# Split value products, transfers to head strips, and a new engine order in six local-attention layers

## The chip, the cores and the metric

The kernel runs on one core of a Trainium2 chip. The core has TensorE (PE in the profile; its weight loads are PEld), VectorE (DVE), ScalarE (ACT), GpSimd (POOL) and SyncE (SP), which here only issues transfers. Each has its own instruction stream, and they meet at semaphores. The metric is device time in microseconds of one launch.

## The reference

A layer norm of x (2 sequences of 1024 rows, 128 wide) feeds two branches, whose results are added to x. One is a causal attention with 8 heads over 2 latent key/value groups (the global attention). The other is six local layers, one after the other. Cut to what matters, a local layer is:

```
qkv = shift_tokens(x) @ Wqkv                      # 128 -> 3 * 1024, 16 heads of 64
q, k = l2norm(q) * qs, l2norm(k) * ks             # then rotary, with a scale that grows with the row
sim = 8 * q . k                                   # a block of 32 rows sees its own block and the one before
attn = softmax(where(mask, -max, sim))
x = (attn @ v).reshape(b, n, 1024) @ Wo + x
xn = layernorm(shift_tokens(x)) * g + b
a, gate = split(xn @ W1 + b1)                     # 128 -> 2 * 341
x = (a * gelu(gate)) @ W2 + b2 + x
```

## The kernel before

All data of a sequence lies in SBUF. The global attention comes first (some 270 us); then a loop over steps G runs the six local layers, 16 tiles of 128 rows each, as a pipeline: each engine has its own list of functions that it calls in step G, each for a tile G - 1, G - 2 and so on, and every wait is a semaphore written by hand. The order inside each list is the order of calls in the last loop of each engine's block. A few functions work on chunks of four tiles: `chunk_at(G, 10)` names the chunk whose turn it is in step G, so the feed-forward's work falls in steps 10 to 13 after the chunk began, and recurs every four steps.

A tile passes these stations. TensorE projects queries and keys (`projected`: each 512 columns are three matmuls, upper x upper, upper x lower, lower x upper, of fp32r parts). ScalarE squares them (`square_keys`, `square_queries`), VectorE multiplies by the rotary tables `tabs` (`cosine`, `sine`) and sums the squares; POOL adds the two rotary parts, makes the seeds of the inverse roots (`seeds`, `refine`), and scales (`scale_keys`, `scale_queries`). TensorE transposes keys, queries and later the probabilities through banks 2 and 3 (`transposes`), ScalarE copies them out. `scores` adds the products onto a mask in banks 4 and 5, VectorE takes maxima and subtracts them, ScalarE exponentiates, VectorE sums, POOL scales.

Values. The weights of values and output are folded for each layer into M (`products`, `folded_upper`), so that the values of a head are already 128 wide. `values(k, g)` makes 64 of a tile's 128 rows in each of two calls: 32 rows at a time, the four heads' groups q land on the four partition strips of 32 in banks 4 and 5, in plain fp32. So ScalarE's `copy_values` puts them in `vw` where `weigh` needs them: strip q holds heads of group q, a block of 32 rows in the free dimension. `vw` is a ring of six half tiles.

Keys. `kT` holds 32 columns of look-back ahead of the tile's 128; POOL's `lookback` copies the last 32 to the front for the next tile.

Rows of the feed-forward. VectorE's `attended` adds the attention to the residual `Xt`; SyncE's `rows_in_place` moves these rows, one half shifted down by one row, to `lns` in three transfers; VectorE's `moments` takes their statistics and `normalise_rows` writes `lnx`; TensorE transposes it (`ln_columns`), ScalarE copies it twice (`xnf`, and `xnH` rounded), POOL subtracts (`lower_columns`). `up_gate`, `up_value`, `gelu`, `gated` and `down` are the feed-forward. The gelu needs another activation table than Ln and Exp, so that ScalarE loads tables before and after.

SyncE's list is one queue. In the local layers it holds, for each tile, the three transfers of rows, and for each layer the weights.

## Time and profile before

| | us |
|---|---|
| median of 3 runs | 1753.11 |
| lowest, highest | 1746.89, 1754.92 |
| the profiled execution | 1745.55 |
| its span, first to last instruction | 1743.9 |
| busy in it: TensorE, VectorE | 1619.5, 1495.5 |
| busy in it: POOL, ScalarE | 1340.6, 1318.4 |
| mean granted TensorE clock | 0.984 |

Busy is the time in which an engine had at least one instruction in work; a matmul's end is modelled. The rows further down are from the profiled execution. A step of the pipeline is one tile on each engine.

### The profile page before, as it was taken

To read this page: it belongs to the slowest core of one execution; us is meant where nothing else is said; L and a number is where in the kernel's file an instruction comes from. 1 tells how busy PE (TensorE), PEld (TensorE's weight loads), DVE (VectorE), ACT (ScalarE), POOL (GpSimd) and SP (SyncE) were. 2 spreads that over 40 slices of the span, in tenths; PEclk is the share of its full clock that TensorE was granted. 3 is DMA by queue.
4 is the path that set the end of the run, shared out by engine and by line. 5 is a ranking of instruction groups with operands and counts; after the bars stand their busy time and mean duration, and the time that the engine had idled before them with its cause. 6 is when DMAs were issued, how large, how long until landed. Compare 5 with 4: busy or idle time off the path is not lost.

```text
span 1743.9 us, 72603 instructions
## 1 busy us (share of the span) xinstructions
PE 1619.5 (93%) x31192; PEld 1098.7 (63%) x31192; DVE 1495.5 (86%) x1863; ACT 1318.4 (76%) x1934; POOL 1340.6 (77%) x1311
## 2 busy tenths in 40 slices
PE   6999978889999999999998999999999999999995
PEld 4777855556566666665665666666666666666654
DVE  5677857999889998898998888999999988999982
ACT  3788846687787788778777877877887887788773
POOL 2312159888988899988888888899888998888871
PEclk8999989999999999999999999999999999999997
DMA  5221100100001000011000010000010000000001
GB/s 158 67 50 39 38 1 30 35 7 8 15 7 59 6 8 12 16 31 34 8 12 14 8 57 7 7 12 15 7 59 7 12 6 15 8 7 7 8 7 28
DMA packets 47997, 40.61 MB, mean 23 GB/s; under 512 B 33216, under 2 KB 41152, under 8 KB 46016
## 3 DMA queue, kind: packets, MB, share of 16 engines
q1 hardware_dynamic: 47680, 35.98, 7.4%
q8 instruction: 249, 4.08, 0.9%
q14 instruction: 68, 0.56, 0.1%
HBM read 20.22 MB, written 1.05 MB: 12 GB/s over the span
## 4 chain that ended last, share of the span: by engine, by line
PE 51%; DVE 22%; issue 13%; ACT 8%; POOL 6%; DMA 0%; SPq 0%; DVEq 0%; POOLq 0%; ACTq 0%
PE banks L1205 23%; PE banks L1494 9%; PE banks L1443 5%; PE banks L1518 4%; DVE arena L1066 4%; PE banks L1479 4%; PE banks L1335 4%; DVE lnx L1128 3%; DVE small L1095 3%; DVE small L1101 2%; DVE small L1089 2%; DVE small L1113 2%; DVE arena L1061 2%; ACT arena L807 1%; ACT L873 1%
## 5 line engine op out<-in xcount | busy, mean ns | idle before, releaser
L1494 PE MATMUL banks<-M,xs 128*32 128x512 f32 x3072 | 368.0, 596 | 0.6 <-ACT arena L807 0.3
L1061 DVE TENSOR_TENSOR arena<-banks,tabs 128x1024 f32<-128x1024 f32 x192 | 233.8, 1218 | 35.5 <-ACT arena L767 22.4
L548 POOL TENSOR_TENSOR arena<-arena 128x1024 f32<-128x1024 f32 x96 | 229.8, 2393 | 43.7 <-DVE arena L1066 43.3
L807 ACT ACTIVATE arena<-banks 128x1024 f32<-128x1024 f32 x192 | 197.0, 1026 | 68.3 <-PE banks L1494 67.6
L1066 DVE TENSOR_TENSOR arena<-banks,tabs 128x1024 f32<-128x1024 f32 x192 | 233.2, 1215 | 0.0
L553 POOL TENSOR_TENSOR arena<-arena 128x1024 f32<-128x1024 f32 x96 | 228.3, 2378 | 0.0
L543 POOL TENSOR_TENSOR prob<-prob,small 128x1024 f32<-128x1024 f32 x96 | 184.0, 1916 | 30.0 <-DVE small L1103 30.0
L1128 DVE SCALAR_TENSOR_TENSOR lnx<-lns,small 128x128 f32<-128x128 f32 x96 | 175.3, 1826 | 34.2 <-POOL small L596 32.8
L1205 PE MATMUL banks<-qkH,xsH 128*128 128x512 f32 x384 | 173.1, 451 | 32.1 <-DVE arena L1066 29.2
L1518 PE MATMUL banks<-arena 128*32 128x128 f32 x6144 | 190.9, 277 | 5.6 <-ACT arena L873 4.2
L608 POOL TENSOR_TENSOR arena<-arena,small 128x1024 f32<-128x1024 f32 x96 | 182.9, 1906 | 9.8 <-POOL arena L553 0.4
L602 POOL TENSOR_TENSOR arena<-arena,small 128x1024 f32<-128x1024 f32 x96 | 182.9, 1905 | 7.5
L767 ACT ACTIVATE arena<-banks 128x1024 f32<-128x1024 f32 x96 | 98.3, 1024 | 113.6 <-PE banks L1205 113.4
L1479 PE MATMUL banks<-arena 64*32 64x64 f32 x12288 | 147.2, 226 | 32.0 <-issue 17.0
L1518 PEld LDWEIGHTS banks<-arena 128*32 128x32 f32 x6144 | 164.5, 111 | 12.4 <-issue 6.0
L1479 PEld LDWEIGHTS banks<-arena 64*32 64x32 f32 x12288 | 130.1, 105 | 58.4 <-issue 56.8
L1494 PEld LDWEIGHTS banks<-M,xs 128*32 128x32 f32 x3072 | 88.4, 110 | 123.2 <-issue 116.2
L1205 PEld LDWEIGHTS banks<-qkH,xsH 128*128 128x128 f32 x384 | 73.2, 191 | 132.8 <-issue 110.0
L1205 PE MATMUL banks<-qkL,xsH 128*128 128x512 f32 x384 | 153.6, 400 | 2.4 <-issue 2.4
L1205 PE MATMUL banks<-qkH,xsL 128*128 128x512 f32 x384 | 153.7, 400 | 0.0
L778 ACT ACTIVATE arena<-banks 128x1024 f32<-128x1024 f32 x96 | 98.4, 1025 | 72.0 <-PE banks L1205 71.8
L1443 PEld LDWEIGHTS banks<-cst,arena 64*128 64x128 f32 x3072 | 111.5, 139 | 61.8 <-issue 41.9
(134 smaller groups left out, 3645.4 us busy)
## 6 DMA issues: line engine op xcount, KB each, us to landing
qkraw<-in_wqk_dram SPq DMA_DIRECT2D x6, 1024.0 KB, 5.2
arena<-in_wvo_dram SPq DMA_DIRECT2D x5, 1024.0 KB, 5.4
gq<-w1w SPq DMA_DIRECT2D x64, 64.0 KB, 2.0
lns<-Xt SPq DMA_DIRECT2D x96, 32.0 KB
lns<-Xt SPq DMA_DIRECT2D x96, 31.8 KB
xsH<-w1w SPq DMA_DIRECT2D x32, 64.0 KB, 2.0
xsL<-w1w SPq DMA_DIRECT2D x32, 64.0 KB, 2.0
W<-in_w_dram SPq DMA_DIRECT2D x6, 341.0 KB, 3.2
```

Of the source, the lines that this page charges most:

```text
L543: pool.tensor_tensor(p, p, d, ALU.mult).then_inc(s["p_nrm"], 1)
L548: pool.tensor_tensor(kc, kc, ks, ALU.add).then_inc(s["k_add"], 1)
L553: pool.tensor_tensor(qc, qc, qs, ALU.add).then_inc(s["q_add"], 1)
L807: act.activation(vw[:, (2 * k + g) % RV, :], two(V_BANK), ACT.Copy).then_inc(s[f"v_cp{g}"], 1)
L1061: dve.tensor_tensor(heads(c), heads(two(0)), table(k % NT, kind), ALU.mult).then_inc(s[done], 1)
L1066: dve.tensor_tensor(w.rearrange("p (h z k) -> p h z k", h=LH, z=2), swapped(two(0)), table2(k % NT, kind + 1), ALU.mult).then_inc(s[done], 1)
L1128: dve.scalar_tensor_tensor(lnx[:, :], lns[:, k % 2, :], ag[:, k % 2, 0:1], rs[:, 4, 32:33].to_broadcast([P, D]), ALU.subtract, ALU.mult).t ...
L1205: return pe.matmul(o, l, r, start=start, stop=stop)
L1443: ins = pe.transpose(bk(2 + o)[:, 64 * k:64 * (k + 1)], src[r, P * k:P * (k + 1)], ident[r, r])
L1479: ins = pe.matmul(bk(4 + o)[WIN * w:WIN * (w + 1), 64 * j:64 * (j + 1)], qT[r, j, WIN * w:WIN * (w + 1)], kT[r, j, WIN * w:WIN * w + 64], ...
L1494: ins = pe.matmul(bk(V_BANK + z)[WIN * q:WIN * (q + 1), :], xs[:, b, t0:t0 + WIN], M[:, q, :, :].rearrange("p m n -> p (m n)"), start=True ...
L1518: ins = pe.matmul(bk(PV_BANK)[WIN * w:WIN * (w + 1), 0:D], ptile[:, NQ * z + m, WIN * w:WIN * (w + 1)], block_of(k, w - 1 + z)[:, D * m:D ...
```

## The change

It moves several things at once, all in the local layers.

Values: the folded weights are kept as an upper and a lower fp32r part (MH, and ML in the place of a buffer of the global attention); VectorE's `folded_lower` makes the lower part. `values(k, g)` now makes all 128 rows of half of the head groups, in six matmuls of 128x512. Its result has rows on partitions, so ScalarE copies it to `vst`, and SyncE moves it to the strips of `vw` by 16 transfers a tile, each of 32 partitions and 2 KB a partition (`place_values`). `weigh` waits for these.

```diff
             def values(k, g):
...
+                pe.wait_ge(s["xs_L"], k // 4 + 1)
+                pe.wait_ge(s["M_L"], 2 * (k // TILES) + 2)
                 claim(V_BANK, V_BANK + 1)
+                xH, xL = xsH[:, b, P * i:P * (i + 1)], xsL[:, b, P * i:P * (i + 1)]
                 for z in range(2):
-                    t0 = P * i + 64 * g + WIN * z
-                    for q in range(NQ):
-                        ins = pe.matmul(bk(V_BANK + z)[WIN * q:WIN * (q + 1), :], xs[:, b, t0:t0 + WIN],
-                                        M[:, q, :, :].rearrange("p m n -> p (m n)"), start=True, stop=True, skip_group_check=True)
+                    mH, mL = (a[:, 2 * g + z, :, :].rearrange("p m n -> p (m n)") for a in (MH, ML))
+                    mm(bk(V_BANK + z), xH, mH, True, False)
+                    mm(bk(V_BANK + z), xH, mL, False, False)
+                    ins = mm(bk(V_BANK + z), xL, mH, False, True)
...
             def copy_values(k, g):
                 act.wait_ge(s[f"v_mm{g}"], k + 1)
-                after(act, "o_mm", k - 2 + g)
-                act.activation(vw[:, (2 * k + g) % RV, :], two(V_BANK), ACT.Copy).then_inc(s[f"v_cp{g}"], 1)
+                if k:
+                    act.wait_ge(v_in[g], P * k)
+                act.activation(vst[:, g, :], two(V_BANK), ACT.Copy).then_inc(s[f"v_cp{g}"], 1)
...
+            def place_values(k, g):
+                if k <= LAST_TILE:
+                    sp.wait_ge(s[f"v_cp{g}"], k + 1)
+                    after(sp, "o_mm", k - 1)
+                    for q in range(2 * g, 2 * g + 2):
+                        for w in range(NW):
+                            sp.dma_start(block_of(k, w)[WIN * q:WIN * (q + 1), :], vst[WIN * w:WIN * (w + 1), g, CH * (q % 2):CH * (q % 2 + 1)])\
+                              .then_inc(v_in[g], 16)
...
+            def folded_lower(l, r):
+                dve.wait_ge(s["M_H"], 2 * l + r + 1)
+                m = [a.rearrange("p q (o r) n -> p o q r n", r=2)[:, :, :, r, :] for a in (MH, ML)]
+                dve.tensor_tensor(m[1], two(2).rearrange("p (o q n) -> p o q n", o=2, q=NQ), m[0], ALU.subtract).then_inc(s["M_L"], 1)
```

The transposes that share banks 2 and 3 with the folded weights now wait for M_L in the place of M_H. SyncE's order in a tile becomes:

```diff
+                place_values(k + 2, 0)
                 rows_in_place(k)
+                place_values(k + 2, 1)
+                load_table(k + 3)
```

`load_table` fetches one piece of the rotary table anew in the second half of each layer, since the table is now scaled in place and has no copy (this makes room for `vst`).

Rows and columns of the feed-forward: the normalisation goes from VectorE to ScalarE, with a small product (`row_shifts`) on POOL ahead of it; the lower part of the columns goes from POOL to VectorE, which reads the bank, so that the copy `xnf` is gone.

```diff
+            def normalise_rows(k):
+                if is_tile(k):
+                    act.wait_ge(s["row_mr"], k + 1)
+                    after(act, "lnB_mm", k)
+                    act.activation(lnx[:, :], lns[:, k % 2, :], ACT.Identity, bias=nmr[:, k % 2:k % 2 + 1], scale=rs[:, 4, 32:33])\
+                       .then_inc(s["ln_x"], 1)
...
-                    dve.scalar_tensor_tensor(lnx[:, :], lns[:, k % 2, :], ag[:, k % 2, 0:1],
-                                             rs[:, 4, 32:33].to_broadcast([P, D]), ALU.subtract, ALU.mult).then_inc(s["ln_x"], 1)
+            def lower_columns(k):
+                if is_tile(k):
+                    at, f = k % 4 * P, k // 4 % 2
+                    dve.wait_ge(s["xn_H"], k + 1)
+                    dve.tensor_tensor(xnL[f][:, at:at + P], bk(6)[:, 0:P], xnH[f][:, at:at + P], ALU.subtract).then_inc(s["xn_L"], 1)
```

Keys: `kT` becomes a ring of six blocks of 32; `scores` reads pairs of neighbouring blocks from it (`key_pair`), and POOL's copy is gone, but for clearing one block at the start of a sequence.

The orders of the lists: the three gate projections of a chunk come in the same step and use banks 6, 7, 7, the three gelus follow each other on ScalarE between one pair of table loads, `moments` goes from the head of VectorE's step to its end, and `weigh` and `values_lower` go from the head of TensorE's step to the end of the one before, which changes nothing in the row of instructions.

```diff
-LAST_GELUS = (1, 2,)
+GATE_BANK, VALUE_BANK = (6, 7, 7), (6, 7, 6)
+LAST_GELU = 2
```

TensorE, from the transpose of the normalised rows to the scores of a tile, in a step with projections up. `cst,lnx` is that transpose, `cst,arena` that of the queries, `cst,prob` that of the probabilities. Before:

```order
L1536 MATMUL banks<-cst,lnx 128x128
L1443 MATMUL banks<-cst,arena 128x64 x16
L1494 MATMUL banks<-M,xs 32x512 x8
L1205 MATMUL banks<-xnw,w1w 128x512 x3
L1443 MATMUL banks<-cst,prob 128x64 x16
```

Now (`gq` is ML, and `w1w` here is the fourth quarter of the columns):

```order
L1600 MATMUL banks<-cst,lnx 128x128
L1498 MATMUL banks<-cst,arena 128x64 x16
L1260 MATMUL banks<-MH,xsH 128x512
L1260 MATMUL banks<-gq,xsH 128x512
L1260 MATMUL banks<-MH,xsL 128x512
L1260 MATMUL banks<-MH,xsH 128x512
L1260 MATMUL banks<-gq,xsH 128x512
L1260 MATMUL banks<-MH,xsL 128x512
L1260 MATMUL banks<-xnw,w1w 128x512 x2
L1260 MATMUL banks<-w1w 128x512
L1498 MATMUL banks<-cst,prob 128x64 x16
```

The values' half went from eight matmuls of 32 rows to six of 128, and both kinds are followed by the feed-forward's products as before.

SyncE, in the middle of a layer, where a new sequence begins (`zrow` is its empty row). Before, two tiles:

```order
L354 DMA lns<-Xt 127x64 [waits ln_x,x1]
L358 DMA lns<-zrow 1x16x4 [waits zeroed]
L359 DMA lns<-Xt 128x64
L354 DMA lns<-Xt 127x64 [waits ln_x,x1]
L358 DMA lns<-Xt 1x16x4
```

Now, one tile with a table piece behind it:

```order
L414 DMA arena<-vst 32x512 [waits o_mm,v_cp0]
L414 DMA arena<-vst 32x512 x7
L359 DMA lns<-Xt 127x64 [waits ln_x,x1]
L363 DMA lns<-Xt 1x16x4
L364 DMA lns<-Xt 128x64
L414 DMA arena<-vst 32x512 [waits o_mm,v_cp1]
L414 DMA arena<-vst 32x512 x7
L405 DMA tabs<-in_tab_dram 128x256 [waits tab,q_s]
```

The three transfers of rows stand between two groups of eight, and a piece of the table behind them.

ScalarE, around the gelus. L873 and L910 are `gelu`, L767 and L796 `square_keys`, L802 and L833 `copy_probs`. Before (the third gelu has a pair of loads of its own, at the end of the step):

```order
L802 ACTIVATE arena<-banks 128x1024
L873 ACT_TABLE_LOAD
L873 ACTIVATE arena<-banks,b1p 128x512
L767 ACTIVATE arena<-banks 128x1024
L873 ACTIVATE arena<-banks,b1p 128x512
L876 ACT_TABLE_LOAD
L840 ACTIVATE prob<-prob 128x1024
```

Now:

```order
L910 ACT_TABLE_LOAD
L910 ACTIVATE arena<-banks,b1p 128x512
L833 ACTIVATE arena<-banks 128x1024
L910 ACTIVATE arena<-banks,b1p 128x512
L796 ACTIVATE arena<-banks 128x1024
L910 ACTIVATE arena<-banks,b1p 85x512
L913 ACT_TABLE_LOAD
```

All three gelus stand between two loads, from the end of one step to the head of the next.

## Rows read from the trace of the kernel before

**Rows 1.** The page: busy us of each engine, and the chain that ended last.

```profile
PE 1619.5 (93%) x31192; PEld 1098.7 (63%) x31192; DVE 1495.5 (86%) x1863; ACT 1318.4 (76%) x1934; POOL 1340.6 (77%) x1311
...
PE 51%; DVE 22%; issue 13%; ACT 8%; POOL 6%; DMA 0%; SPq 0%; DVEq 0%; POOLq 0%; ACTq 0%
```

**Rows 2.** Busy us by window: PE, PEld, DVE, ACT, POOL, then clock, DMA, GB/s.

```profile
500.00:750.00 250.00, 241.02 (x4899) 158.23 (x4892) 231.67 (x272) 202.35 (x264) 223.64 (x215) 1.00 0.07 18
```

**Rows 3.** Timeline (start, duration, instruction), VectorE: first tile, and 80 tiles later.

```profile
276.60 0.28 DVE L1108 TENSOR_TENSOR Xt<-banks,Xt 128x128 f32<-128x128 f32 x1
...
1499.44 0.28 DVE L1108 TENSOR_TENSOR Xt<-banks,Xt 128x128 f32<-128x128 f32 x1
```

**Rows 4.** Timeline of TensorE through one step of the local layers.

```profile
589.81 1.90 PE L1494 MATMUL banks<-M,xs 128*32 128x512 f32 x16
591.64 0.50 PE L1205 MATMUL banks<-qkH,xsH 128*128 128x512 f32 x1
...
593.14 0.27 PE L1536 MATMUL banks<-cst,lnx 128*128 128x128 f32 x1
...
593.98 1.92 PE L1494 MATMUL banks<-M,xs 128*32 128x512 f32 x16
595.83 2.94 PE L1205 MATMUL banks<-W,arena 128*128 128x128 f32 x24
...
602.27 0.60 PE L1582 MATMUL banks<-cst,Xt 128*128 128x128 f32 x4
...
605.22 0.61 PE L1494 MATMUL banks<-M,xs 128*32 128x512 f32 x4
```

**Rows 5.** Timeline of TensorE, one up projection.

```profile
580.87 0.96 PE L1205 MATMUL banks<-xnw,w1w 128*128 128x512 f32 x3
```

**Rows 6.** Groups: count, busy us, mean ns, then idle before and its releaser.

```profile
L548 POOL TENSOR_TENSOR arena<-arena 128x1024 f32<-128x1024 f32 x96 | 229.8, 2393 | 43.7 <-DVE arena L1066 43.3
...
L1128 DVE SCALAR_TENSOR_TENSOR lnx<-lns,small 128x128 f32<-128x128 f32 x96 | 175.3, 1826 | 34.2 <-POOL small L596 32.8
...
L1119 DVE TENSOR_TENSOR prob<-banks,small 128x1024 f32<-128x1024 f32 x96 | 117.6, 1225 | 10.3 <-DVE small L1113 0.5
...
L873 ACT ACT_TABLE_LOAD x46 | 59.0, 1283 | 2.3 <-PE banks L1205 1.5
...
L559 POOL TENSOR_TENSOR xnw<-xnf,xnw 128x128 fp32r<-128x128 f32 x96 | 44.1, 459 | 5.0 <-ACT xnw L854 5.0
...
L570 POOL COPY arena<-arena 128x256 f32<-128x256 f32 x84 | 38.0, 452 | 9.2 <-PE banks L1479 8.9
...
L1108 DVE TENSOR_TENSOR Xt<-banks,Xt 128x128 f32<-128x128 f32 x96 | 26.9, 281 | 7.3 <-PE banks L1518 7.2
...
L853 ACT ACTIVATE xnf<-banks 128x128 f32<-128x128 f32 x96 | 26.1, 271 | 5.2 <-PE banks L1536 5.2
```

**Rows 7.** Timeline of VectorE at the end of the kernel.

```profile
1724.05 0.34 DVE L1128 SCALAR_TENSOR_TENSOR lnx<-lns,small 128x128 f32<-128x128 f32 x1
```

**Rows 8.** Timeline of SyncE's queue in the global attention: 16 transfers, and 16 more.

```profile
167.44 2.41 SPq L371 DMA_DIRECT2D xsH<-w1w  x4
169.90 3.23 SPq L371 DMA_DIRECT2D xsL<-w1w  x4
173.17 5.02 SPq L371 DMA_DIRECT2D gq<-w1w  x8
182.21 2.41 SPq L371 DMA_DIRECT2D xsH<-w1w  x4
...
187.19 6.12 SPq L371 DMA_DIRECT2D gq<-w1w  x8
```

**Rows 9.** Timeline of SyncE's queue in a local layer: the rows of one tile.

```profile
608.89 0.63 SPq L354 DMA_DIRECT2D lns<-Xt  x1
...
610.46 0.59 SPq L359 DMA_DIRECT2D lns<-Xt  x1
```

**Rows 10.** The page, DMA issues: count, KB each, us from issue to landing.

```profile
gq<-w1w SPq DMA_DIRECT2D x64, 64.0 KB, 2.0
```

More of the change, by code:

```diff
@@ L125, in build @@
         xs = sb("xs", [P, B, T + 1])
-        xnw = sb("xnw", [P, 4 * CH], F32R)
-        xnH, xnL = (xnw[:, 2 * CH * i:2 * CH * (i + 1)].rearrange("p (f n) -> p f n", f=2) for i in range(2))
-        M = sb("M", [P, NQ, NQ, D])
+        xnw = sb("xnw", [P, 3 * CH], F32R)
+        quarters = [xnw[:, CH * i:CH * (i + 1)] for i in range(3)] + [w1w[:, 4 * FF:4 * FF + CH]]
+        xnH, xnL = quarters[0:2], quarters[2:4]
+        MH = sb("MH", [P, NQ, NQ, D], F32R)
         gq2 = sb("gq2", [P, 2, T], F32R)
-        gK = [xnw[:, T * z:T * (z + 1)] for z in range(2)]
+        ML = gq2.rearrange("p z t -> p (z t)").rearrange("p (q m n) -> p q m n", q=NQ, m=NQ)
+        vst = sb("vst", [P, 2, 2 * CH])
+        gK = [quarters[0:2], quarters[2:4]]
         gQ = [xsH[:, 1, 0:T], xsL[:, 1, 0:T], gq2[:, 0, :], gq2[:, 1, :]]
@@ L153, in build @@
         gag = small[:, 466:498].rearrange("p (t k) -> p t k", k=2)
+        nmr = small[:, 498:500]
         lns = sb("lns", [P, 2, D])
@@ L223, in build @@
         rows_in = [sem("rows_in0"), sem("rows_in1")]
+        v_in = [sem("v_in0"), sem("v_in1")]
         lat_w, lat_wq, lat_k, out_in = (sem(n) for n in ("lat_w", "lat_wq", "lat_k", "out_in"))
@@ L389, in _, with load_table @@
                     place_queries(it, z)
+            sp.wait_ge(s["gK_lo"], 2 * B * KV)
+            sp.wait_ge(s["gQ_lo"], 2 * B * KV)
+            sp.dma_start(tabs[:, NT // 2:NT, :], tab_d[:, NT // 2:NT, :]).then_inc(tab_in, 16)
+            def load_table(k):
+                l, n = divmod(k, TILES)
+                if 0 <= k <= LAST_TILE and n >= NT and l + 1 < DEPTH:
+                    sp.wait_ge(s["q_s"], k + 1)
+                    sp.wait_ge(s["tab"], NT * (l + 1) + n - NT)
+                    sp.dma_start(tabs[:, n - NT, :], tab_d[:, n - NT, :]).then_inc(tab_in, 16)
+            def place_values(k, g):
[6 more added lines that the diff above has]
+                              .then_inc(v_in[g], 16)
             out_t = out.rearrange("b (t p) d -> p (b t) d", p=P)
+            for k in range(2):
+                for g in range(2):
+                    place_values(k, g)
             for k in range(LAST_TILE + 1):
@@ L787, in copy_keys @@
                     act.wait_ge(s["kT_mm"], k + 1)
-                    act.wait_ge(s["look"], k + 1)
-                    act.activation(kT[:, :, WIN:WIN + P].rearrange("p k (o t) -> p k o t", o=2), halves(2), ACT.Copy)\
-                       .then_inc(s["kT_cp"], 1)
+                    after(act, "s_mm", k)
+                    first = NW * k % KB // 2
+                    at = kT.rearrange("p k (o t) -> p k o t", t=2 * WIN)
+                    at = at[:, :, 2::-2, :] if first == 2 else at[:, :, first:first + 2, :]
+                    act.activation(at, halves(2), ACT.Copy).then_inc(s["kT_cp"], 1)
             def copy_queries_T(k):
@@ L1033, in _ @@
             add_outputs(PAIRS - 2)
-            dve.memset(gl[2][64:128, :], 1.0).then_inc(s["ones"], 1)
             dve.memset(rin[:, :, :], 1.0).then_inc(s["ones"], 1)
-            dve.wait_ge(s["ones"], 2)
             def heads(a):
@@ L1133, in moments @@
                     dve.wait_ge(rows_in[k % 2], 48 * (k // 2) + 48)
+                    after(dve, "row_mr", k - 1)
+                    after(dve, "ln_x", k - 1)
                     dve.bn_stats(st6[:, :], lns[:, k % 2, :]).then_inc(s["ln_bn"], 1)
@@ L1510, in weigh @@
                     pe.wait_ge(s["pt_cp"], k + 1)
-                    pe.wait_ge(s["v_cp0"], k + 1)
-                    pe.wait_ge(s["v_cp1"], k + 1)
+                    for g in range(2):
+                        pe.wait_ge(v_in[g], P * (k + 1))
                     pe.wait_ge(s["vw_0"], 1)
@@ L1556, in up_value, with down, down_first @@
                     up(c, j, FJ[j][0], f"a_mm{j}")
-                    freed[6 + j % 2] = (f"h{j}", c + 1)
-            def down(c):
+                    freed[VALUE_BANK[j]] = (f"h{j}", c + 1)
+            def down(c, tiles):
+                for t in tiles:
+                    for j in range(3):
+                        m = FJ[j][1] + (j == 2)
+                        ins = mm(bk(DN_BANK)[:, P * t:P * (t + 1)], gl[j][0:m, P * t:P * (t + 1)], W2[0:m, c // NC % 2, j, :], j == 0, j == 2)
+                return ins
+            def down_first(c):
                 if c is not None:
@@ L1564, in down, with down_last @@
                     claim(DN_BANK)
-                    for t in range(4):
-                        for j in range(3):
-                            m = FJ[j][1] + (j == 2)
-                            ins = mm(bk(DN_BANK)[:, P * t:P * (t + 1)], gl[j][0:m, P * t:P * (t + 1)], W2[0:m, c // NC % 2, j, :], j == 0, j == 2)
-                    ins.then_inc(s["f_mm"], 1)
+                    down(c, (0, 1))
                     freed[DN_BANK] = ("x_new", c + 1)
+            def down_last(c):
+                if c is not None:
+                    down(c, (2, 3)).then_inc(s["f_mm"], 1)
             def next_shifts(c):
```

177 lines of the change are left out of this document (92 added, 85 removed).

## The prediction

> **What bounds the kernel now.** I read the page's busy shares and its chain first [rows 1]. TensorE is busy 93% of the span, VectorE 86%, POOL 77%, ScalarE 76%; the chain that ended last runs through TensorE for 51% of the span, through VectorE for 22%, and another 13% is "issue". So no engine alone sets the pace. TensorE does it for most of the time and VectorE where TensorE has to wait for it.
>
> Then the stages. In 250 us from the middle of the local layers [rows 2] TensorE works 241.0, VectorE 231.7, POOL 223.6, ScalarE 202.4. Three engines are within 7% of the stretch. The pace itself is read from the addition that ends the attention of a tile (VectorE L1108, once a tile): it starts at 276.60 for the first tile and at 1499.44 five layers of 16 tiles later [rows 3]. That is 1222.84 / 80 = 15.3 us a tile, on average. The local layers fill some 1460 of the 1744 us; what lies ahead (the global attention) is hardly touched by the change.
>
> What TensorE must do in a tile is read off one full step of its program, from the lower values at 589.81 to the next ones at 605.22 [rows 4]: 15.41 us without a hole. In it lie the down projection (2.94 us) and the layer transposes (0.60 us), which come once in four tiles; since the end of a group runs 0.07 us into the next one (591.64 against 589.81 + 1.90), they occupy 2.87 and 0.53 us; without them a step holds 12.0 us. One up projection is 0.96 - 0.07 = 0.89 us [rows 5], and six come in four tiles. So a tile costs 12.0 + (2.87 + 0.53 + 6 x 0.89) / 4 = 14.2 us on average, and the weight products and bias columns at a layer's edge (about 3.5 us in 16 tiles, an estimate from the 24 small products of the down projection in 2.87 us) make it 14.4. Against 15.3 that leaves **0.9 us a tile in which TensorE waits**.
>
> **The change part by part.**
>
> Values. The two halves of a tile's values take 591.64 - 589.81 = 1.83 and 595.83 - 593.98 = 1.85 us now [rows 4]. The new code makes each half of six 128x512 products on the same operands' shapes and types as a projection, and a projection of six takes 593.14 - 591.64 = 1.50 us. So TensorE gains 0.33 + 0.35 = 0.68 us a tile: 96 x 0.68 = **65 us**, all of it on the engine that sets the pace. New TensorE content: 14.4 - 0.7 = 13.7 us a tile.
>
> VectorE. L1128 leaves it: 1826 ns on average, 175 us in all [rows 6]. Its size (128x128) is that of L1108 at 281 ns [rows 6], so most of it is standing still. At the very end of the kernel, where POOL has nothing left, it takes 0.34 us [rows 7]; I read the rest as a wait for POOL. The new L1164 (lower part of the normalised columns) has one operand in PSUM and is of the form of L1108: 0.28 us. The lower parts of the folded weights add 12 instructions of the size of L1119, 1.2 us each, 0.15 us a tile. VectorE goes from 231.7 / 250 x 15.3 = 14.2 us a tile to 14.2 - 1.83 + 0.28 + 0.15 = **12.8**.
>
> POOL loses L559 (459 ns) and 84 copies of L570 (452 ns, 0.40 us a tile) and gets a one-column instruction that no row shows; it lies between 0 and the 0.46 of L559, and I take 0.25: 223.6 / 250 x 15.3 = 13.7 goes to **13.1**. ScalarE loses the second copy of the columns (L853, 271 ns) and gets the normalisation of a 128x128 tile: the same size, so nothing. The table loads fall from 92 around the gelus to 46: 46 x 1.283 = 59 us [rows 6], 0.6 us a tile, so ScalarE goes from 12.4 to **11.8**. That counts above all in the step that held all three gelus and four loads.
>
> The Trainium skill, ScalarE: Activation LUTs, section "What ACT_TABLE_LOAD costs", puts a switch to another set at 2.66 us, the load of 1283 ns with a drain of 1380 ns. The load agrees with this trace (1283 ns); for the drain the trace has no row. By the page 46 switches would be 122 us of ScalarE, by the rows 59.
>
> SyncE gets the real bill: 16 transfers of 64 KB a tile, where it had three small ones. The global attention issues exactly that pattern (16 transfers, 32 partitions by 2 KB): 167.44 to 178.19 and 182.21 to 193.31 [rows 8], so 10.75 and 11.1 us, **0.68 us each** with the long one among them. The three row transfers last from 608.89 to 611.05, 2.2 us [rows 9]. A table piece in every second tile and the weight loads add 0.3 + 0.25 us. Together 10.9 + 2.2 + 0.55 = 13.7 us a tile. It fits below 14.3, with little to spare, and it does not run ahead: the first eight wait for the ScalarE copy of the lower half, the second eight stand behind the rows, which wait for the residual addition. Laid out by hand from the order of the program and the durations above, with the end of the query projection as 0: lower half copied at about -0.3, its eight issued by 5.3, rows by 7.5, upper eight by 13.0, table piece by 13.6. The statistics of those rows now stand at the end of VectorE's step, at about 13, and the rows have landed by 10 (a 64 KB transfer lands in 2.0 us [rows 10]); the weighing that needs the values comes some 8 us after they landed. So SyncE's own work is hidden as long as one issue stays at 0.68. The transfers themselves move 1 MB in 14 us; in the global attention the same 1 MB went in 11 [rows 8], so bandwidth is not the matter.
>
> What is late next. With VectorE and ScalarE relieved, TensorE waits for POOL's chain (rotate, scale, seeds), which is 13.1 of 14.3 us. Three gate projections now lie in one step and one in the next (TensorE's four steps become 11.3 + 2.7 = 14.0, 11.3 + 0.9 = 12.2, 11.3 + 1.8 = 13.1 and 11.3 + 3.4 = 14.7 us), so in the light step POOL or SyncE paces and in the heavy ones they catch up. I take a third of the 0.9 us of waiting as gone: 0.3 us in 80 tiles, **24 us**. The bounds are nothing (0) and nearly all of it (0.75 x 80 = 60).
>
> Costs of the edges. Before the transposes at a layer's edge TensorE used to wait for ScalarE's copy of the folded weights; now VectorE's lower part comes behind it, 1.2 us, and about 1 us of it shows: 5 us. At the entry two such instructions and the first transfers: 3 to 5 us, taken as 4. The ring of key blocks takes the place of POOL's copy with no instruction of its own; the key copy keeps its size. Bounds of these small things: -2 to +15 us.
>
> Sum: 65 + 24 - 5 - 4 = 80. The profiled execution took 1745.55 us (span 1743.9), so 1745.6 - 80 = **1666 us**. That execution is 0.4% below the median 1753.11; the shown runs reach from 1746.9 to 1754.9, and I keep to the profiled one.
>
> **The rivals.**
>
> All waiting goes. If the 0.9 us were nearly all VectorE's doing (the chain gives it 22%), TensorE runs through: 1745.6 - 65 - 60 + 5 = 1626 us. Against it: POOL at 13.1 and SyncE at 13.7 do not let 13.7 through evenly.
>
> SyncE paces, mildly. If an issue costs 0.72 to 0.77 us in this traffic, SyncE needs 11.5 to 12.3 + 2.75 = 14.3 to 15.1 us and the tile follows it: 1680 to 1740 us. For it: the rows put it at 13.7 already, and each handshake (copy done, residual done) adds some tenths that the global attention didn't have.
>
> SyncE paces, and the kernel gets slower. One group of four in the trace took 3.23 us (0.81 each) [rows 8]. If that were the usual price, 16 x 0.81 + 2.75 = 15.7 us, and with some 0.4 us of handshakes 16.1: 0.8 us a tile over now, 77 us, **about 1820 us**. It decides from 15.3 us a tile, that is from about 0.76 us an issue with the handshakes. Place: the second eight stand behind the rows on SyncE, then ScalarE's upper copy waits for their landing and TensorE for that copy. Against it: only one in eight to sixteen issues was long in the global attention.
>
> The change does nothing. POOL's chain of 13.1 us plus its waits for k_s and the denominators would hold 15.2 us; then 1740 to 1750. Little speaks for it, since POOL's largest idle, 43.7 us before L548, ends with VectorE's L1066 [rows 6], and VectorE comes earlier now.
>
> **How the numbers follow.** Forecast as summed, 1640 to 1695 us: 0.50. All waiting gone, 1610 to 1640: 0.12. SyncE mildly, 1695 to 1740: 0.20. Same: 0.05. Slower: 0.13. What a measurement of this kernel can tell from no change is about 0.5%. So faster 0.82, same 0.05, slower 0.13. The range 1622 to 1740 leaves out the slower case, the same and the end of the best one.
>
> **What would show it.** In the profile after: six value products in 1.5 us between starts; L1128's 175 us gone from VectorE and the new lower columns at about 0.28 us; 46 table loads fewer; 16 transfers issued in about 11 us a tile on SyncE, with a short idle behind them; the addition after attention every 14.3 us. The forecast is wrong if TensorE or ScalarE waits for the landing of values (v_in), if VectorE's statistics wait for rows, or if the light step (one gate product, the third in four) is as long as the others.

## The result, and the profile after

The changed kernel takes 1766.07 us (median of 5 runs, 1763.87 to 1768.14) against 1753.11 before. The ratio of runs made side by side is 1.008, with a 95% interval of 1.0061 to 1.010: slower by 0.8%, where 1666 us was forecast with a range of 1622 to 1740. The profiled execution took 1768.14 us, its span is 1766.4, and the mean granted TensorE clock is 0.964 (0.984 before).

The page of the changed kernel, to be held against [rows 1]: busy us of each engine, the chain that ended last, and the granted clock in 40 slices.

```profile
PE 1592.2 (90%) x29272; PEld 1260.5 (71%) x29272; DVE 1363.8 (77%) x1875; ACT 1274.8 (72%) x1888; POOL 1294.2 (73%) x1227
...
PEclk8999998999999999999999999999999999999997
...
PE 70%; ACT 10%; issue 9%; DVE 4%; POOL 3%; SPq 3%; DMA 1%; ACTq 0%; POOLq 0%; DVEq 0%
```

Every engine has less to do: TensorE 27 us less, VectorE 132, POOL 46, ScalarE 44. TensorE's share of the chain rose from 51 to 70% and VectorE's fell from 22 to 4%. So the relief is there, and the profiled span is still 22.5 us longer. The same stretch as [rows 2] (PE, PEld, DVE, ACT, POOL busy, clock, DMA share, GB/s):

```profile
500.00:750.00 250.00, 233.10 (x4622) 185.30 (x4607) 205.97 (x265) 192.21 (x255) 214.02 (x197) 0.99 0.37 91
```

TensorE works 233 of 250 us where it had worked 241. Where it stands, the groups say (count, busy us, mean ns, then the idle time ahead and what ended it). First the scores in the kernel before:

```profile
L1479 PE MATMUL banks<-arena 64*32 64x64 f32 x12288 | 147.2, 226 | 32.0 <-issue 17.0 <-ACT banks L822 11.9
```

and in the changed one, with the weighing, the normalisation, the lower columns, a table load and the copy of the values:

```profile
L1582 PE MATMUL banks<-arena 128*32 128x128 f32 x6144 | 198.7, 284 | 2.1 <-DVE arena L1202 1.5 <-issue 0.4
...
L839 ACT ACTIVATE vst<-banks 128x1024 f32<-128x1024 f32 x192 | 196.7, 1025 | 75.6 <-PE banks L1260 71.7 <-DMA arena<-vst 3.5
L1542 PE MATMUL banks<-arena 64*32 64x64 f32 x12288 | 162.9, 227 | 90.7 <-issue 48.9 <-ACT banks L854 41.6
...
L890 ACT ACTIVATE lnx<-lns,small 128x128 f32<-128x128 f32 x96 | 46.1, 480 | 0.8 <-POOL small L598 0.7
...
L910 ACT ACT_TABLE_LOAD x23 | 29.5, 1283 | 0.4
...
L1164 DVE TENSOR_TENSOR xnw<-banks,xnw 128x128 fp32r<-128x128 f32 x48 | 13.5, 281 | 2.2 <-ACT xnw L884 2.2
```

Idle ahead of a score product went from 32.0 to 90.7 us. It has two parts. 41.6 us end with L854, ScalarE's copy of the mask into banks 4 and 5: TensorE is at the scores before the mask is. And 48.9 us are "issue": TensorE stands in the middle of the 128 products of a tile and waits for no engine. One such place, in the timeline of the changed kernel's TensorE (start, duration, instruction):

```profile
1284.02 0.39 PE L1260 MATMUL banks<-qkH,xsL 128*128 128x512 f32 x1
1284.25 0.39 PE L1260 MATMUL banks<-qkH,xsH 128*128 128x512 f32 x1
...
1288.79 0.71 PE L1498 MATMUL banks<-cst,prob 64*128 64x64 f32 x16
1289.92 1.42 PE L1542 MATMUL banks<-arena 64*32 64x64 f32 x109 [0.41 <-ACT banks L854]
1293.82 0.60 PE L1542 MATMUL banks<-arena 64*32 64x64 f32 x19 [2.49 <-issue]
1294.35 0.79 PE L1260 MATMUL banks<-qkH,xsH 128*128 128x512 f32 x1
1294.94 0.63 PE L1260 MATMUL banks<-qkL,xsH 128*128 128x512 f32 x1
1295.37 0.63 PE L1260 MATMUL banks<-qkH,xsL 128*128 128x512 f32 x1
```

The probabilities' transposes, then 0.41 us for the mask, 109 score products in 1.42 us, a stop of 2.49 us, the other 19. Behind the stop the same projection product comes every 0.43 us where it came every 0.23 us ahead of it (1284.02, 1284.25). The windows ahead of and behind the stop:

```profile
1281.00:1285.00 4.00, 4.00 (x56) 3.16 (x45) 4.00 (x5) 3.94 (x6) 3.44 (x2) 1.00 0.36 86
...
1293.80:1297.20 3.40, 3.38 (x26) 2.56 (x27) 2.45 (x2) 0.00 (x0) 3.04 (x2) 0.51 0.36 81
```

The granted clock went from 1.00 to 0.51, the upper and the lower of the two levels of 2.4 and 1.2 GHz. I counted both from the records of the local layers. Stops of over 0.3 us within the scores: 14 with 17.0 us before, 25 with 48.9 us after. Stretches at the lower clock: 3 with 10.2 us together before, 19 with 71.7 us after; ahead of 17 of these 19 TensorE had just stood for over 0.9 us. Half of 71.7, some 36 us, is my estimate of the time lost there, against 5 us before.

The last place is SyncE's queue (timeline, changed kernel): eight transfers of values, then the rows of one tile; the next eight transfers stand behind these.

```profile
1303.51 5.91 SPq L414 DMA_DIRECT2D arena<-vst  x8
1309.51 0.66 SPq L359 DMA_DIRECT2D lns<-Xt  x1
1310.22 0.84 SPq L363 DMA_DIRECT2D lns<-Xt  x1
1311.10 1.05 SPq L364 DMA_DIRECT2D lns<-Xt  x1
```

Eight in 5.91 us are 0.74 us each here; over all 1536 the mean is 0.65 (median 0.59, and 124 of them over 0.9 us). In a steady stretch SyncE is occupied about 14.2 of 15.5 us a tile, the short pauses between issues counted in (13.1 us in the issues alone). ScalarE waited 3.5 us in the whole kernel for landed values (L839 above).

### The profile page after: what moved, and what is told of

The parts are those of the page before. It is cut to its first block, busy times and chain, and to the rows that moved or that the text cites. A ratio compares the mean times of both kernels' runs of the same rounds, so it can differ in the third digit from the quotient of the medians.

```text
span 1766.4 us, 70552 instructions
## 1 busy us (share of the span) xinstructions
PE 1592.2 (90%) x29272; PEld 1260.5 (71%) x29272; DVE 1363.8 (77%) x1875; ACT 1274.8 (72%) x1888; POOL 1294.2 (73%) x1227
## 4 chain that ended last, share of the span: by engine, by line
PE 70%; ACT 10%; issue 9%; DVE 4%; POOL 3%; SPq 3%; DMA 1%; ACTq 0%; POOLq 0%; DVEq 0%
PE banks L1260 41%; PE banks L1582 9%; PE banks L1542 8%; PE banks L1498 7%; PE banks L1390 4%; ACT vst L839 4%; ACT banks L854 3%; SPq L414 2%; POOL arena L631 1%; POOL arena L586 1%; POOL arena L637 1%; DMA arena<-vst 1%; DVE gq L1169 0%; DVE small L1131 0%; PE banks L1600 0%
## 5 line engine op out<-in xcount | busy, mean ns | idle before, releaser
L1149 DVE TENSOR_REDUCE small<-banks 128x16 f32<-128x1024 f32 x96 | 117.6, 1225 | 185.1 <-PE banks L1542 185.1
L796 ACT ACTIVATE arena<-banks 128x1024 f32<-128x1024 f32 x96 | 98.5, 1027 | 216.5 <-PE banks L1260 216.4
L839 ACT ACTIVATE vst<-banks 128x1024 f32<-128x1024 f32 x192 | 196.7, 1025 | 75.6 <-PE banks L1260 71.7
L1542 PE MATMUL banks<-arena 64*32 64x64 f32 x12288 | 162.9, 227 | 90.7 <-issue 48.9
L1542 PEld LDWEIGHTS banks<-arena 64*32 64x32 f32 x12288 | 142.6, 106 | 104.8 <-issue 100.8
L576 POOL TENSOR_TENSOR prob<-prob,small 128x1024 f32<-128x1024 f32 x96 | 184.3, 1919 | 31.8 <-DVE small L1139 31.5
L1582 PE MATMUL banks<-arena 128*32 128x128 f32 x6144 | 198.7, 284 | 2.1 <-DVE arena L1202 1.5
L1260 PE MATMUL banks<-MH,xsH 128*128 128x512 f32 x384 | 172.4, 449 | 0.5 <-ACT vst L839 0.5
L1260 PE MATMUL banks<-MH,xsL 128*128 128x512 f32 x384 | 152.0, 396 | 0.0
L1260 PE MATMUL banks<-gq,xsH 128*128 128x512 f32 x384 | 151.5, 395 | 0.0
L1498 PE MATMUL banks<-cst,arena 64*128 64x64 f32 x3072 | 142.8, 235 | 7.3 <-POOL arena L631 3.0
```

The lines of the kernel that those rows point to most:

```text
L576: pool.tensor_tensor(p, p, d, ALU.mult).then_inc(s["p_nrm"], 1)
L839: act.activation(vst[:, g, :], two(V_BANK), ACT.Copy).then_inc(s[f"v_cp{g}"], 1)
L1260: return pe.matmul(o, l, r, start=start, stop=stop)
L1498: ins = pe.transpose(bk(2 + o)[:, 64 * k:64 * (k + 1)], src[r, P * k:P * (k + 1)], ident[r, r])
L1542: ins = pe.matmul(bk(4 + o)[WIN * w:WIN * (w + 1), 64 * j:64 * (j + 1)], qT[r, j, WIN * w:WIN * (w + 1)], key_pair(r, j, NW * k + w - 1), ...
L1582: ins = pe.matmul(bk(PV_BANK)[WIN * w:WIN * (w + 1), 0:D], ptile[:, NQ * z + m, WIN * w:WIN * (w + 1)], block_of(k, w - 1 + z)[:, D * m:D ...
```

## The experiments

All were timed beside the kernel before; its medians were 1751.35 us beside e1, e3 and e4, 1749.01 beside e5 to e8 and 1752.15 beside e9 to e12. In the table "stops" and "mask" are the idle us ahead of a score product that end with "issue" and with the mask copy, from the groups of each profile, and "low clock" is the us of local layers at the lower level. The ratios carry the comparisons between rows; e8, e9, e10 and e12 were run four times each, the others nine or ten times. The last three columns are from one execution of each kernel, and some of these lie off the median: e3's took 1773.59 us, e5's 1733.04, e8's 1717.74, e9's 1778.37, e10's 1777.22 and e11's 1745.71.

| | median us | ratio to before [95%] | stops | mask | low clock |
|---|---|---|---|---|---|
| before | | 1 | 17.0 | 11.9 | 10.2 |
| changed | 1766.07 | 1.008 [1.0061, 1.0100] | 48.9 | 41.6 | 71.7 |
| e1 no transfers | 1747.75 | 0.9969 [0.9937, 1.0001] | 45.3 | 37.5 | 68.3 |
| e3 old values | 1760.96 | 1.0039 [1.0012, 1.0067] | 31.2 | 44.8 | 61.4 |
| e4 padding | 1766.18 | 1.0079 [1.0055, 1.0104] | 51.6 | 38.5 | 81.9 |
| e5 tiny transfers | 1748.11 | 0.9987 [0.9956, 1.0019] | 32.7 | 38.9 | 44.4 |
| e6 old gates | 1748.37 | 0.9984 [0.9959, 1.0009] | 39.1 | 23.1 | 51.2 |
| e7 old values, old gates | 1755.74 | 1.0033 [1.0012, 1.0053] | 26.7 | 19.9 | 37.5 |
| e8 transposes first | **1725.54** | **0.987 [0.9815, 0.9926]** | 17.4 | 35.5 | 30.7 |
| e9 before, adjacent | 1771.29 | 1.0102 [1.0052, 1.0153] | 25.9 | 15.5 | 23.9 |
| e10 before, first | 1785.3 | 1.0186 [1.0134, 1.0237] | 21.2 | 11.3 | 27.3 |
| e11 old values, first | 1750.57 | 0.9996 [0.9965, 1.0026] | 19.6 | 35.9 | 34.1 |
| e12 no transfers, first | 1710.22 | 0.9771 [0.9726, 0.9816] | 20.3 | 29.2 | 37.5 |

The first question was whether the 16 transfers, the new values or the rest of the change took the gain.

**e1: the changed kernel without the transfers.** ScalarE copies straight into `vw`. The values then stand in the wrong strips; what each engine computes keeps its size.

```diff
             def copy_values(k, g):
...
-                act.activation(vst[:, g, :], two(V_BANK), ACT.Copy)
+                after(act, "o_mm", k - 2 + g)
+                act.activation(vw[:, (2 * k + g) % RV, :], two(V_BANK), ACT.Copy)
...
-                place_values(k + 2, 0)
                 rows_in_place(k)
-                place_values(k + 2, 1)
```

> The changed kernel without the 16 transfers a tile: ScalarE copies the values straight to the ring, so the rows of the values stand in the wrong strips (the output is not the reference's); TensorE's matmuls are the same in number and size. Two things may have cost the forecast gain. Theory SyncE: issuing and landing of the transfers (TensorE's waits ahead of the scores grew from 5.5 to 33.8 us, and ScalarE's staging copies wait for landings). Theory pauses: TensorE stops in the middle of the score matmuls right behind a 16 KB fetch of its instructions (9 stops, 17 us before; 19 stops, 46 us after) and runs at half clock for 3.4 us after each (3 such stretches before, 19 after). If SyncE alone: the 28 us and what hangs on it go, 1766 to about 1735, and the stops stay at 19. If the stops come from the traffic of the transfers: they fall to 9 or fewer and the time to 1670 to 1685, near the forecast of 1666. If the stops come from where fetches fall in the instruction stream: they stay, whatever the transfers.

1747.75 us, 18 less than the changed kernel. The transfers cost something, but without them 65 us of TensorE's work and the relief of three engines are still worth only 0.3%, with an interval that just reaches nothing. Stops and mask waits are nearly those of the changed kernel, and 21 of the 25 stops come in the same tile at the same product. They belong to the program, not to the transfers.

**e3: the changed kernel with the values of before** (plain fp32, no transfers, no lower parts of the folded weights).

```diff
-                    mm(bk(V_BANK + z), xH, mH, True, False)
-                    mm(bk(V_BANK + z), xH, mL, False, False)
-                    ins = mm(bk(V_BANK + z), xL, mH, False, True)
+                    t0 = P * i + 64 * g + WIN * z
+                    for q in range(NQ):
+                        ins = pe.matmul(bk(V_BANK + z)[WIN * q:WIN * (q + 1), :], xs[:, b, t0:t0 + WIN],
+                                        M[:, q, :, :].rearrange("p m n -> p (m n)"), start=True, stop=True, skip_group_check=True)
```

> The changed kernel with the values of before (plain fp32, 32 rows at a time, straight into the ring; no folded lower parts, no transfers): all the rest of the change alone. By the forecast's terms the rest (rows on ScalarE, key ring, gelus grouped) brings 24 us of TensorE's waiting and costs nothing at the edges: about 1725 to 1730. If the rest of the change is at fault (order of the gates, key ring), it is at 1750 or more. Theory pauses by the place in the stream: the instruction count of a tile is that of before again, so the number of stops returns to about 9.

1760.96 us. The rest of the change alone costs some 7 us by the ratio (10 by the medians), where I had it as a gain of 24. So the new values with all that belongs to them cost 7 us on top (ratios 1.0080 and 1.0039; 5 by the medians), in place of giving 65.

**e4: 128 waits that are already fulfilled, on TensorE ahead of the local loop.** If the stops came from where the program's pieces happen to begin, shifting it would change their number.

```diff
+            for _ in range(128):
+                pe.wait_ge(s["xs_L"], 1)
             for G in range(STEPS):
                 project_queries(G - 1)
```

> The changed kernel with 128 already fulfilled semaphore waits on TensorE ahead of the local loop, at its start: this shifts all later fetches of its instructions against the matmuls, and costs 5 us or less once. If the stops in the scores depend on where a fetch falls in the stream, their number and the time move clearly (by 10 us or more, either way). If they come from the traffic of transfers, both stay: 19 stops, 1766 to 1771 us.

1766.18 us, the time of the changed kernel. The stops moved to other products, mostly of other tiles, and their sum stayed (51.6 against 48.9 us). So the position in the stream decides which product is hit, but an unlucky position isn't what made them many.

**e5: e1 with 16 tiny transfers a tile**, 32 rows of 64 bytes, with the same waits and semaphores.

```diff
+                            sp.dma_start(dm[WIN * q:WIN * (q + 1), 16 * w:16 * (w + 1)], vw[WIN * w:WIN * (w + 1), (2 * k + g) % RV, CH * (q % 2):CH * (q % 2) + 16])\
+                              .then_inc(v_in[g], 16)
```

> The kernel without transfers, to which 16 tiny ones a tile are added again, each 32 partitions by 64 bytes into a tile that nobody reads, with the same waits for them on ScalarE and TensorE (the values stand in the wrong strips, so the output is not the reference's). SyncE then has the changed kernel's queue, but the megabyte is gone. The kernel without transfers ran in 1747.75 us, the changed one in 1766. If issues and their waits make the 18 us, this is at 1760 to 1768; if the bytes make them (the score matmuls take 1.59 us at the median with transfers, 1.41 without), it is at 1745 to 1752 with scores at 1.41.

1748.11 us, the same as e1 (1747.75), each with some 5 us of uncertainty. So SyncE's issues and their handshakes cost nothing that these runs can tell; the 18 us are the price of the bytes. (e2, a first form of this with the real transfers made narrow, gave no time.)

**e6: the changed kernel with the gates' places of before.** The third gate product comes one step later; it and the third value product stand again between the probabilities' transposes and the scores; the third gelu has its own table loads at the end of the step.

```diff
                 up_value(chunk_at(G, 12), 1)
-                up_value(chunk_at(G, 12), 2)
                 up_gate(chunk_at(G, 10), 0)
...
                 transpose_probs(G - 3)
+                up_value(chunk_at(G, 12), 2)
+                up_gate(chunk_at(G, 11), 2)
                 scores(G - 2)
...
-                up_gate(chunk_at(G, 10), 2)
```

> The changed kernel with the feed-forward's products in the places of before: the third gate one step later, and it and the third value product between the transposes of the probabilities and the scores, on ScalarE the third gelu at the end of the step with table loads of its own. Theory place: with a slow run of products ahead of the scores, TensorE neither waits for the mask at their start (63 waits over 0.3 us in the changed kernel, 38.9 us; 11.9 us before) nor stops so long within them (48.9 against 17.0 us), so it falls to 1700 to 1730 us although ScalarE gets 46 table loads more. Rival: the stops come with the new values (fewer, denser instructions); then it stays within 1750 to 1770, and the table loads cost what little the waits gave.

1748.37 us: 18 less, although ScalarE has 59 us of table loads more again. Both kinds of idle time ahead of score products fell. The regrouping that was to help ScalarE is what costs these 18 us.

**e7: e3 and e6 together.** What is left of the change is the normalisation on ScalarE, the lower columns on VectorE, the statistics at the step's end and the ring of key blocks.

> As the last, but with the values of before too (plain fp32, no transfers): what is left of the change is the rows on ScalarE, the lower columns on VectorE, the key ring and the moved statistics. By the forecast they give about 24 us against the kernel before (1751): 1725 to 1730. If place is what costs in the run with old values alone (1761), this is at or below 1735; if the key ring or the moved statistics cost, it stays at 1750 or more.

1755.74 us, 0.33% over before (0.12 to 0.53). This rest relieves VectorE by 145 us (1350.1 busy) and buys nothing.

**e8: the changed kernel, with only TensorE's order changed.** In the changed kernel the transposes of the probabilities stand directly ahead of the scores. Here they go up, behind the first gate and value product and the first half of the down projection, and the other products of the feed-forward lie between them and the scores, whichever of them the step has.

```diff
                 up_gate(chunk_at(G, 10), 1)
                 up_value(chunk_at(G, 12), 1)
+                down_first(chunk_at(G, 13))
+                transpose_probs(G - 3)
+                down_last(chunk_at(G, 13))
                 up_value(chunk_at(G, 12), 2)
                 up_gate(chunk_at(G, 10), 0)
-                down_first(chunk_at(G, 13))
-                down_last(chunk_at(G, 13))
                 up_value(chunk_at(G, 11), 0)
-                transpose_probs(G - 3)
                 scores(G - 2)
```

> The changed kernel; only TensorE's transposes of the probabilities move ahead of the third value, the first gate and the first value product, so that slow products stand right ahead of the scores in three of four steps; ScalarE's order and the table loads stay as changed. Theory place, part on the instruction stream: the stops within the scores shrink from 48.9 to about 20 us and stretches at half clock from 19 to under 10; waits for the mask stay (the same work lies ahead of the scores). About 1735 us. If earlier transposes wait for POOL's scaled probabilities, some of it is lost; if the stops don't hang on what stands ahead of the scores, 1760 to 1770.

**1725.54 us (1717.74 to 1739.44), 40 less than the changed kernel (37 by the ratios) and 1.3% below the one before**: a version that beats both. Its groups and one step in its timeline of TensorE:

```profile
L1542 PE MATMUL banks<-arena 64*32 64x64 f32 x12288 | 159.7, 226 | 53.2 <-ACT banks L854 35.5 <-issue 17.4
```

```profile
1241.32 0.71 PE L1498 MATMUL banks<-cst,prob 64*128 64x64 f32 x16
1241.96 0.93 PE L1260 MATMUL banks<-xnw,w1w 128*85 128x512 f32 x3
1243.14 1.76 PE L1542 MATMUL banks<-arena 64*32 64x64 f32 x128 [0.25 <-ACT banks L854]
```

Three long products lie between the 16 quick ones and the 128 quick ones, and the 128 run through in one piece. Stops fell from 48.9 to 17.4 us, the value of the kernel before; time at the lower clock from 71.7 to 30.7 us. The mask waits stayed (35.5).

**e9: the kernel before, with only its transposes moved down**, to directly ahead of the scores, as in the changed kernel.

```diff
-                transpose_probs(G - 3)
                 up_value(chunk_at(G, 12), 2)
                 up_gate(chunk_at(G, 11), 2)
+                transpose_probs(G - 3)
                 scores(G - 2)
```

> The kernel before, in which only TensorE's transposes of the probabilities move down by up to two up projections, to stand right ahead of the scores in every step, as in the changed kernel. All else, values and gelus too, is that of before. Theory place: in the changed kernel the stops came with this neighbourhood (32 quick transposes and 256 quick score instructions in a row), so stops in the scores grow from 17 to 35 us or more, stretches at half clock from 3 to 10 or more, and the time from 1750 to 1765 to 1780 us. Rival: the stops belong to the new values; then it stays within 1745 to 1755.

1771.29 us, 19 more than before. This one edit makes the old kernel as slow as the changed one, but the stops are only a part of it: those within the scores rose from 17.0 to 25.9 us, those elsewhere hardly (8.4 to 8.6 in the local layers). The larger part is a wait of another kind, at the third gate product. With the transposes gone from ahead of it TensorE reaches it sooner, and waits for VectorE to have read the bank (`gated`, L1152). The group before, and in e9:

```profile
L1205 PE MATMUL banks<-xnw,w1w 128*85 128x512 f32 x144 | 44.6, 418 | 10.8 <-DVE arena L1152 10.3 <-ACT arena L873 0.5
...
L1205 PE MATMUL banks<-xnw,w1w 128*85 128x512 f32 x144 | 43.5, 411 | 25.6 <-DVE arena L1152 25.1 <-ACT arena L873 0.5
```

That is 15 us more, against 9 of stops and 4 of mask waits. So e9 shows that the place matters in the old kernel too, and supports the stops only weakly.

**e10: the kernel before with e8's idea**, the transposes up behind the first gate and value product. It isn't the same edit: the weight products of the next layer also go up, and a gate and a value product change places with others.

> The kernel before, with TensorE's transposes of the probabilities moved up behind the first gate, so that slow products stand right ahead of the scores in each step: the edit that took the changed kernel from 1766 to 1725.5. If place helps the kernel before as much as it has stops to lose (17 us, 3 stretches), 1730 to 1745. If VectorE's late queue sets its pace, as the forecast read it, the earlier transposes wait for POOL and it stays at 1750 or gets slower.

1785.3 us: what gives 40 us in the changed kernel costs 33 here. The waits of its profile (waiting engine and line, what ended them: us in total, times, longest) name the largest reason, first for the weight loads of the transposes, then for their products:

```profile
PEld banks L1443 <- POOL prob L543: 71.1, 56, 2.6
...
PE banks L1443 <- POOL prob L543: 22.1, 35, 2.2
```

The transposes wait for POOL's scaled probabilities. In the kernel before the loads waited 17.2 us for them in all and the products 3.1; in e8, where VectorE and POOL have been relieved, 39.1 and 11.8 us (L576 there). The products' wait is the one in which TensorE does nothing. Another 8.4 us of e10 are up projections that wait for POOL's lower columns, which e8 no longer has on POOL. So the relief makes the better order possible, as far as e10 is the same order.

**e11 and e12: e8's order with the values of before (the edit of e3), and without transfers (the edit of e1).** They price the new values in an order that stops little.

> The kernel with transposes first (1725.5 us), with the values of before (plain fp32, no transfers). What the new values with their transfers are worth once the stops are few: by matmul time 0.68 us less and about 0.11 (weighing) and 0.17 (scores) us more a tile, 0.4 x 96 = 38 us, less 5 at the edges; so this should be at 1725 + 33 = about 1758 by that, or at 1745 if waits give half of it back. If it is at 1725 or below, the new values bring nothing.

> Transposes first, and the values copied straight to the ring without transfers (rows in the wrong strips, so the output is not the reference's): what the transfers still cost. With the order as changed they cost 18 us (1766 against 1748). If that is slower fetches and score matmuls at 1.58 in place of 1.41 us, it is again 15 to 20: about 1707. If it was mostly stops, less: 1715 to 1722.

1750.57 and 1710.22 us. With this order the new values give 25 us (1750.6 to 1725.5; 22 by the ratios), and they would give 40 without the transfers' bytes (1750.6 to 1710.2). The bytes cost 15 us (17 by the ratios), much as in the other order (18). With so few runs none of these differences is known to better than some 10 us. e11 also says what the relief and the new order are worth without the new values: 0.9996 of the kernel before, nothing. e8's whole gain over the kernel before is that of the new values. Against the old places of the gates (e6, e7) e8's order gives 23 us with the new values and 5 with the old ones.

## Why the prediction was wrong

**The values' term was right.** From the start of a half to the next group it took 1.85 us (median) before and takes 1.51 now: 0.34 us twice a tile, 65 us of TensorE's time. So were the reliefs: VectorE 132 us less (forecast 1.40 x 96 = 134), POOL 46 (forecast 58).

**ScalarE's term was mis-sized.** Normalising there was put down as "the same size, so nothing"; L890 takes 480 ns, not the 271 of L853 that it replaced, 20 us more in all. ScalarE fell by 44 us (59 forecast). The loads themselves cost what the rows said. In the changed kernel's timeline of ScalarE the gelu's first activation starts 1.29 us after its load did:

```profile
1289.85 0.23 ACT L900 ACTIVATE small<-small 128x33 f32<-128x33 f32 x1
1290.10 1.28 ACT L910 ACT_TABLE_LOAD   x1
1291.39 0.69 ACT L910 ACTIVATE arena<-banks,b1p 128x512 f32<-128x512 f32 x1
```

The load starts 0.02 us after the instruction ahead of it ended, and so it is with all 46 loads around the gelus (median 0.02 us idle ahead of a load, 0.01 behind). The 2.66 us of the Trainium skill (ScalarE: Activation LUTs, "What ACT_TABLE_LOAD costs") doesn't show here.

**SyncE's cover held.** Forecast 13.7 us a tile hidden under TensorE's; measured about 14.2 (0.65 us an issue and 0.05 between two, rows 2.3 us), and e5 shows no cost of the issues. The rival with this mechanism had the right side and the wrong cause: the kernel is slower, but not by SyncE. What I got wrong beside it is "bandwidth is not the matter": the bytes cost 15 to 18 us in the two pairs of runs (changed and e1 or e5; e8 and e12).

**The step that failed is the sum on TensorE:** content 14.4 - 0.7, plus 0.9 us of waits of which a third goes. I took the content of a step for a fixed sum and the waits for something that only other engines cause, so that moving products between steps was free ("changes nothing in the row of instructions", and the light step as the only concern). Between starts of groups over 96 tiles, the local layers before and after differ as follows: values -65; scores with their stops +45; weighing +18; projections +6; transposes +6; waits at the start of the scores +27; other waits -14. Together +23, and the span grew by 22.5. The forecast had -65, nothing for the work's other terms, and -24 for the waits.

The waits' term taken by itself, as TensorE's idle time in the local layers by what ended it: VectorE 36 us before and 21 after, POOL 5 and 6, ScalarE 17 and 48, "issue" 25 and 61. The relief took 15 of the 24 us that I had counted on, and the other two kinds, which I had at nothing, gave 66. TensorE's busy time there fell by 26 us and not by 65, since stretches at the lower clock and longer scores and weighings took the rest back.

What a stop is can be read beside the page's queue of instruction transfers (count, MB, share):

```profile
q8 instruction: 235, 3.85, 1.0%
```

These are 235 transfers of 16 KB, about 1.1 us each. TensorE's records (products, weight loads, waits) are 60159, so that a transfer holds 256 of them, 64 bytes each. All 26 "issue" stops of over 0.9 us in the local layers stand at one place of such a piece of 256 (193 or 194 records over a multiple of it), as do 229 of the 232 in all thirteen profiles; with e4's padding they keep that place and hit other products. Each of the 26 ended 1.2 to 1.5 us after a transfer had landed. TensorE had started 221 records (median) in the 2 us ahead of these stops, and 85 in the 2 us ahead of the borders that it passed without one. So in these stops TensorE waits for the next piece of its own instructions, and they come where quick products lead up to its border.

What stands behind the two large terms:

1. *Stops, and the lower clock behind them.* The regrouping put the 16 transposes (0.64 us) directly ahead of the 128 scores (1.41 us) in all four kinds of step, where products had lain between them in two: 144 products in 2 us. e8 takes only that neighbourhood away, and stops and time fall (31.5 and 40 us). Between the profiles of the two, 50 us apart, TensorE's "issue" time in the local layers fell by 32 us and its busy time by 17, while all its other waits together stayed within 3. e9 makes the neighbourhood in all steps of the kernel before, where a part of the cost is this and a larger one a wait for VectorE. How much of e8's 40 us each of the two is, the stop and the clock behind it, no run tells apart.
2. *The mask.* With the gates and the last value product gone from between the transposes and the scores, TensorE arrives at the scores sooner, while ScalarE copies the upper values and only then the mask. These waits grew from 11.9 to 41.6 us, in three of the four kinds of step, not in the light one alone. e6, with products between again, halves them (23.1), and e7 with the old values has 19.9. I had looked for the next late engine at POOL and SyncE. In fact it was ScalarE, the engine with the least to do. That the order of its list makes it late is read from the list; no run changes it alone.

**What stays open.** Why the rest of the change alone (e7) costs 0.3%: its stops and low-clock time are above those of before (26.7 and 37.5 us against 17.0 and 10.2), and TensorE's waits for ScalarE grew there (17 to 29 us) while those for VectorE shrank (36 to 20), which I have only read. How the bytes cost 15 to 18 us: the groups of scores alone take 17 us less in e1's profile than in the changed kernel's and 9 less in e12's than in e8's, but e5's take as long as with the bytes for each tile and cost no time; the instruction transfers take a median of some 1140 ns in the changed kernel, 1080 in e1, 1040 to 1060 in e5 and 1000 before, but in e8 1136 with few stops. Neither settles it. And the remaining mask waits of e8 (35.5 us): copying the mask ahead of the upper values wasn't tried.

## What to carry to other kernels

Before counting on a gain on the engine that sets the pace, look at what a reordering puts next to each other: long runs of quick instructions can cost more in stops and clock than the work that was saved, and moving a few long products between two such runs adds no work. Where engines were relieved and nothing came of it, try other orders; here one gave 40 us against the changed order and 23 against the old places, and nearly the same order harmed the kernel without the relief. When work leaves the place ahead of a group, ask what that group needs next (here a mask copy), and look at the order of the supplier's list, not only at its busy share. And count the waits by who ended them before naming a cause: e9 lost time as expected, mostly by a wait that nobody had expected.

## What was not expected of the hardware

- 128 score products take 1.41 us (median) from start to next group without transfers on SyncE (before, e1, e3, e12) and 1.57 to 1.60 with them (changed, e5, e8), with tiny transfers (e5) as with 64 KB ones. Yet the median of e5 is no slower than e1's; its profiled execution lies 15 us below that median and can't tell why.
- The weighing, 64 products that didn't change, went from 277 to 284 ns a product and from 1.77 to 1.88 us a tile (median) in the changed kernel; with the old values (e3, e7) it stayed at 1.77. It goes with the new values and not with the transfers, since e1 and e12 have 1.88 too; no run tells why.
- A stop of 2.49 us is followed by a granted clock of 0.51 for the 3.4 us shown above, and the products there take twice the time: such a stop costs more than its own length.
